# One group's shared-expert products moved behind the expert pairs, in a two-layer transformer block on one core

## The reference, cut to what matters

```python
def _L0_ffn_ref(x, gate_w, W1, W2, Ws1, Ws2):      # D 256, H 192, E 8, K 2, NS 2
    scores = jax.nn.softmax((xf @ gate_w.T).astype(jnp.float32), axis=-1)
    top_vals, top_idx = jax.lax.top_k(scores, K)
    w_dense = jnp.zeros((T, E), x.dtype).at[jnp.arange(T)[:, None], top_idx].set(weights)
    h = jnp.einsum('td,ehd->teh', xf, W1)
    y, g = jnp.split(h, 2, axis=-1)
    eo = jnp.einsum('teh,edh->ted', y * jax.nn.silu(g), W2)
    z = jnp.einsum('te,ted->td', w_dense, eo)
    z = z + _gated_mlp(xf, Ws1, Ws2)               # the shared expert, hidden width 384
    return z.reshape(x_shape)
x = L0_attn_x                                      # (2, 2048, 256) float32
x = _layernorm(x + _L0_attn_ref(x, L0_attn_w_qkv, L0_attn_w_conv1), axis=-1)
x = _layernorm(x + _L0_ffn_ref(x, ...), axis=-1)
```

## Time and profile before

| | |
|---|---|
| Device time, three runs | 361.57, 362.41, 365.29 us; median 362.41 us |
| Span of the profiled execution | 354.0 us (the time of that execution itself is not printed; the median lies 8.4 us above this span) |
| TensorE busy | 315.3 us, 89% of the span |
| VectorE busy | 265.5 us, 75% |
| ScalarE busy | 192.7 us, 54% |
| GpSimd busy | 197.5 us, 56% |
| Mean granted TensorE clock | 0.962 of full speed |

### The profile page before, as it was taken

One profiled execution on the slowest core, in us unless ns is written; L12 is line 12 of the kernel. 1 busy time (PEld: TensorE's weight loads), 2 busy tenths in 40 slices (PEclk: granted clock), 3 DMA queues, 4 the chain that ended last, 5 costly groups with the idle time before them and its releaser, 6 DMA issues.

```text
span 354.0 us, 7780 instructions
## 1 busy us (share of the span) xinstructions
PE 315.3 (89%) x2225; PEld 282.8 (80%) x2225; DVE 265.5 (75%) x1037; ACT 192.7 (54%) x425; POOL 197.5 (56%) x223
## 2 busy tenths in 40 slices
PE   2879899999999989999989979999999999999700
PEld 1446788789888878888889979999999999999600
DVE  0886679866989897966686765676678886988785
ACT  1043686646657362733335644555655566868862
POOL 4048750746778858667271542444757675686620
PEclk9969999999999999999999998999999999999955
DMA  7967420212371202442124643444899797789758
GB/s 221 378 220 262 126 62 0 95 47 75 101 216 58 92 33 93 114 136 101 35 98 140 191 144 100 129 131 131 178 247 204 202 243 190 177 236 252 204 189 324
DMA packets 31383, 54.63 MB, mean 154 GB/s; under 512 B 4880, under 2 KB 22544, under 8 KB 31344
## 3 DMA queue, kind: packets, MB, share of 16 engines
q1 hardware_dynamic: 23136, 29.82, 28.1%
q0 software_dynamic: 8208, 24.32, 23.9%
HBM read 29.73 MB, written 24.40 MB: 153 GB/s over the span
## 4 chain that ended last, share of the span: by engine, by line
PE 48%; DVE 16%; DMA 12%; SPq 8%; POOL 6%; issue 4%; ACT 4%; POOLq 0%; DVEq 0%; ACTq 0%
PE bank L1062 15%; PE bank L946 10%; PE bank L1088 8%; PE bank L968 4%; DMA stage<-ws_t 4%; PE bank L931 3%; PE bank L1071 3%; DMA stage<-rows_in 3%; PE bank L1031 3%; DVE xs L1174 3%; DVE htlo L1379 2%; SPq L415 2%; DVE mix L1374 2%; POOL rows_in L560 2%; POOL w1lo L516 2%
## 5 line engine op out<-in xcount | busy, mean ns | idle before, releaser
L600 POOL DMA_INDIRECT rows_out<-stage,place x71 | 69.4, 977 | 67.2 <-ACT stage L769 51.8
L560 POOL DMA_INDIRECT rows_in<-x,slot x64 | 65.3, 1020 | 47.1 <-DVE slot L1289 30.6
L749 ACT ACTIVATE stage<-bank 128x384 f32<-128x384 f32 (+1 forms) x36 | 17.5, 486 | 43.7 <-PE bank L1062 43.7
L1062 PE MATMUL bank<-w1hi,xthi 128*128 x142 | 39.8, 362 | 1.3 <-DVE xs L1385 1.1
L769 ACT ACTIVATE stage<-bank,weight 128x256 f32<-128x256 f32 x71 | 30.0, 471 | 15.8 <-PE bank L1088 15.7
L1062 PE MATMUL bank<-w1hi,xtlo 128*128 x142 | 36.9, 341 | 0.0
L1062 PE MATMUL bank<-w1lo,xthi 128*128 x142 | 36.8, 340 | 0.0
L1391 DVE TENSOR_TENSOR xtlo<-bank,xthi 128x512 fp32r<-128x512 f32 (+1 forms) x36 | 24.3, 676 | 13.7 <-ACT xthi L695 13.4
L1519 DVE TENSOR_TENSOR stage<-bank,stage 128x384 f32<-128x384 f32 (+1 forms) x36 | 19.8, 551 | 18.6 <-ACT stage L749 18.5
L687 ACT ACTIVATE mix<-bank 128x512 f32<-128x512 f32 x24 | 14.2, 591 | 34.1 <-PE bank L946 34.1
L946 PE MATMUL bank<-xthi,ws1hi 128*128 128x512 f32 x96 | 31.3, 407 | 0.0
(11 more groups left out here) (242 smaller groups left out, 893.4 us busy)
## 6 DMA issues: line engine op xcount, KB each, us to landing
stage<-rows_in SPq DMA_DIRECT2D x71, 133.0 KB, 2.6
xs<-rows_out POOLq DMA_DIRECT2D x12, 512.0 KB, 6.5
xs<-x SPq DMA_DIRECT2D x8, 512.0 KB, 9.2
out<-xs SPq DMA_DIRECT2D x7, 512.0 KB, 5.4
stage<-w_t SPq DMA_DIRECT2D x8, 384.0 KB, 4.4
rows_in<-clear SPq DMA_DIRECT2D x16, 133.0 KB
rows_out<-stage,place POOLq DMA_INDIRECT x71, 3.3
stage<-w_t SPq DMA_DIRECT2D x2, 512.0 KB, 3.9
```

The source lines that it names most:

```text
L560: pool.indirect_dma_start(rows_in[0:E * CAP, :], bass.IndirectOffsetOnAxis(slot[:, q * G + t, k:k + 1], 0), x2[q % 2][:, t, :], None).then ...
L600: pool.indirect_dma_start(rows_out[:, :], bass.IndirectOffsetOnAxis(place[:, 2 * j + b:2 * j + b + 1], 0), by[j % 4][:, b * C:(b + 1) * C] ...
L749: act.activation(bsg[j % 2][:, 0:width(j)], bank_h[j % 2][:, 0:width(j), H:F], ACT.Silu).then_inc(s_bsg, 1)
L1062: mm = pe.matmul(bank_h[j % 2][:, b, 0:F], bx[j % 2][:, (2 * b + k) * P:(2 * b + k + 1) * P], w[:, bass.ds(e, 1), k, :], start=(a == 0), s ...
```

## The change

Of group 7 only the routing stays ahead of the pairs. Its shared-expert products come after the last pair.

```diff
+LAST = NG - 1
-HIDDEN = 2
+HIDDEN = 4
+TABLE_AT = 4
     # TensorE
-            for g in range(NG):
+            for g in range(LAST):
                 group(g)
+            pe.wait_ge(s_xt, NG)
+            block_transposes(0)
+            logits_of(LAST)
+            block_transposes(1)
+            pe.wait_ge(s_pack, 1)
+            load_experts(0)
             pe.wait_ge(s_wlo, PIECES)
-            pe.wait_ge(s_slot, NG)
     # in its step
-                    if j == 2:
+                    if j == TABLE_AT:
                         spread_table(1)
                     if j == 1:
-                        for u in range(2):
-                            pe.wait_ge(s_zev[u], NG)
+                        pe.wait_ge(s_lsum, NG)
+                if i == 1:
+                    places(LAST)
+                    for u in range(2):
+                        pe.wait_ge(s_zev[u], LAST)
+                    if j == 0:
+                        pe.wait_ge(s_slot, NG)
             pairs(step)
+            last_group()
+            def last_group():
+                for m in range(MC):
+                    first_layer(LAST, m)
+                for m in range(2):
+                    pe.wait_ge(s_ht, hidden(LAST, m) + 1)
+                    for t in range(G):
+                        second_layer(LAST, t, [m])
+                close_group(LAST)
     # VectorE, before the pairs
+            block_lo(0)
+            route(LAST)
+            block_lo(1)
     # in its step
+                    if i == 1:
+                        tables(LAST)
+                        slots(LAST)
+                if i == 1:
+                    rest_blocks()
+                if i == 2:
+                    rest_regions()
                 if i == 3:
+                    rest_rows()
+                if i == TABLE_AT + 1:
                     pack_experts(slice(FULL // 4, NBK // 4))
+            def rest_blocks():
+                vec.wait_ge(s_slot, NG)
+                vec.tensor_copy(zrow[:], begin[0:1, :]).then_inc(s_ends, 1)
     # VectorE, behind the pairs
-            statistics(5, 1)
+            product(LAST, 0)
+            hidden_lo(LAST, 0)
+            scale_and_shift(2)
+            product(LAST, 1)
+            hidden_lo(LAST, 1)
+            gather(0)
+            product(LAST, 2)
+            hidden_lo(LAST, 2)
             statistics(6, 0)
-            scale_and_shift(2)
+            add_routed_input(LAST, 0)
             statistics(6, 1)
+            gather(1)
             scale_and_shift(3)
-            statistics(7, 0)
-            statistics(7, 1)
+            statistics(LAST, 0)
+            add_routed_input(LAST, 1)
+            statistics(LAST, 1)
             scale_and_shift(4)
     # ScalarE, behind the pairs
             finish_tiles(halves(3, 1))
-            deviations(2)
-            finish(4)
-            deviations(3)
+            for m in range(MC):
+                silu(LAST, m)
+                hidden_hi(LAST, m)
+                if m:
+                    finish_tiles(halves(4, m - 1))
+            act.preload_act_table(ACT.Sqrt)
             finish(5)
     # GpSimd
-                    26: (4, 1), 28: (5, 0), 30: (5, 1)}
+                    26: (4, 1), 28: (5, 0), 30: (5, 1), 32: (6, 0), 35: (6, 1)}
+            rough_rstd2(2)
+            rough_rstd2(3)
     # SP
-            store_groups(range(3))
+            store_groups(range(4))
             for u in range(2):
-                sp.wait_ge(s_zev[u], NG)
-            for n in range(2):
-                load_last(n, closed_pairs(NG - 1))
-            load_last(2, closed_pairs(HALF))
-            load_last(3, PAIRS)
-            store_groups([3, 4, 5, 6])
+                sp.wait_ge(s_zev[u], LAST)
+            load_last(0, closed_pairs(HALF))
+            load_last(1, PAIRS)
+            store_groups(range(4, LAST))
```

More of the change, by code:

```diff
@@ L224, in post_norm_layer, with last_results, sg, prod @@
         ln2 = [ln2t[:, n] for n in range(5)]
[L225 to L229, removed]
+        def last_results(h, k):
+            return mix[:, 2 * h + k, :].rearrange("p (t c) -> p t c", c=C)
+        def sg(g, m):
+            return work[:, m * GT:(m + 1) * GT] if g == LAST else mix[:, buf(g, m), :]
+        def prod(g, m):
+            return work[:, at_sg + m * GT:at_sg + (m + 1) * GT] if g == LAST else mix[:, 2 + buf(g, m), :]
         tokf = tok[:].rearrange("p b t -> p (b t)")
@@ L339, in buf, with gated, shared, logit_bank @@
             return hidden(g, m) % 2
+        def gated(g, m):
+            return (2 + 2 * m if m < 2 else 0) if g == LAST else 4 + 2 * buf(g, m)
+        def shared(g, u):
+            return (6 if g == LAST else 4 + 2 * buf(g, 1)) + u
+        def logit_bank(g):
+            return banks[5] if g == LAST else banks[2]
+        def place_bank(g):
+            return banks[7] if g == LAST else banks[2]
         def result(j, b):
@@ L711, in _ @@
                 silu(g, 1)
-                if g != 1 and g + 1 < NG:
+                if g != 1:
                     normalise(g + 1)
@@ L940, in first_layer @@
                     pe.wait_ge(s_row0, 1)
-                for h, (o, bank) in enumerate (((m * P, banks[4 + 2 * buf(g, m)]), (HS + m * P, banks[5 + 2 * buf(g, m)]))):
-                    if m == 0 and g:
+                for h, o in enumerate((m * P, HS + m * P)):
+                    bank = banks[gated(g, m) + h]
+                    if m == 0 and 0 < g < LAST:
                         pe.wait_ge(s_zev[h], g)
@@ L1442, in group @@
                     token_max(1)
-                if g + 1 == NG:
-                    vec.wait_ge(s_slot, NG)
-                    vec.tensor_copy(zrow[:], begin[0:1, :]).then_inc(s_ends, 1)
                 if g:
@@ L1562, in statistics, with gather @@
                 ins.then_inc(s_var, 1)
+            def gather(h):
+                tiles = slice(LAST * G + 2 * h, LAST * G + 2 * h + 2)
+                for k in range(K):
+                    before = xs[:, tiles, :] if k else x2[LAST % 2][:, 2 * h:2 * h + 2, 0:C]
+                    vec.wait_ge(s_last_in[h][k], 16)
+                    vec.tensor_tensor(xs[:, tiles, :], before, last_results(h, k), ALU.add).then_inc(s_last_x[k], 1)
+                    vec.wait_ge(s_last_x[k], h + 1)
             def scale_and_shift(n):
```

102 lines of the change are left out of this document (42 added, 60 removed).

## The result

| | changed | before | ratio |
|---|---|---|---|
| median of 4 runs each, us | 372.47 (370.98 to 378.58) | 362.14 (361.57 to 365.29) | 1.0265 [1.0213, 1.0316] |

The change makes the kernel 2.7% slower. Forecast were 363.0 us and a range to 367.0; it failed. Five further sets, each on one chip, came in two conditions.

What follows compares the result with a forecast made beforehand. Bound by TensorE in the pairs, then by a tail writing, reloading, adding and norming the last rows. Pairs end at 327.1 (7.9 us earlier) plus a 27.5 us tail: span 354.6, plus 8.4: 363.0 us, range 357 to 367.

Steps and rivals of the forecast that it cites:

- the front gives 7.9: Ahead of the pairs: pair 4's first load, and so the pairs' end, comes 7.9 us earlier, not 12.5.
- E: The end of the pairs' last matmul, 335.06 in the trace before, forecast at 327.1 after the change.
- both ways: Step from span to time: the median's 8.4 us above the span is added alike for both kernels.
- Part one: How much earlier the pairs end: SyncE's load list lets only 7.9 us of 12.5 through, TensorE idling at pairs 4 and 8.
- TensorE idle before them: Sign of being right: TensorE idles before the transposes of pair 8, near 202, forecast at 3.5 us.
- Part two: The tail behind the last pair's matmuls: follows VectorE's order and grows from 18.9 to 27.5 us.
- third rival: Tail: GpSimd's accumulating transfers land after over 9 us, delaying VectorE's wait for the power; 367.0 to 369.3 us, chance 0.17.
- The lower clock behind 2 us of idle: Tail: TensorE's last chunk takes 2.8 us for 1.4, VectorE's add waits 0.5 us; time would be 363.5.
- The front gives all: Rival at the front: pairs 0 and 8 start the full 12.5 us earlier; 358.4 us, chance 0.09.
- the tail follows TensorE: Rival in the tail: VectorE keeps up, so TensorE's 12.5 us of matmuls set the end; 354.8 us, chance 0.1.
- Late accumulating transfers: Rival in the tail: GpSimd's accumulating transfers land after over 9 us; 367.0 to 369.3 us, chance 0.17.
- The second table or the scatters hold up pair 8: Rival before pair 8's load: these come late despite 6.5 us of margin, each microsecond beyond costing one; chance 0.03.

Runs made afterwards that it cites:

- before_early: The kernel before, with SyncE loading pairs 4 and 5 ahead of its wait for the last group's counts; 360.31 us, 1.0023 of the kernel before.
- before_second: The kernel before, unchanged, run again for its profile in the slower condition; 363.0 us, 1.0024, span 362.0.
- loads_behind: The changed kernel, with SyncE waiting for all of group 7's scatters before pair 4's load instead of pair 8's; 378.11 us, 1.0435 of the kernel before.
- places_first: The changed kernel, with group 7's positions, tables, slots and `zrow` ahead of the first pair instead of in step 1; 369.65 us, 1.0217 of the kernel before.
- after_fourth: The changed kernel, unchanged, run a fourth time; 368.88 us, 1.0243 of the kernel before.
- early_loads: The changed kernel, with SyncE loading pairs 4 and 5 ahead of its wait for the last group's counts; 350.05 us, 0.9885 of the kernel before.
- early_rows2: early_loads, with the rest of the table's rows made in VectorE's step 2 instead of step 3; 348.59 us, 0.9868 of the kernel before.
- best_both: early_rows2, with GpSimd's power ahead of its last accumulating transfer and VectorE's step needing it behind all three low parts; 364.48 us, 1.014 of the kernel before.

## Why the prediction was wrong

**The step that failed: "the front gives 7.9".** Within the condition of the first result the front gives nothing. On set 3's chip E is 339.42 in before_early, which takes as long as the kernel before, and 340.72 in the change: minus 1.3 us. The tail takes 9.4 there (28.50 for 19.10), near the 8.5 of the forecast. In set 1 the same two terms are 8.8 (E 332.76 and 323.93) and 12.2 (30.46 for 18.25).

**How the sum came to miss it: its base.** "The profiled execution's own time is not printed; with the median's 8.4 above the span both ways." The 8.4 puts the kernel before where it was measured, and with 1.8 in its place the forecast would have been 356.4, further from 372.47. What is wrong is "both ways": the part of it inside the span is 8 to 11 us in the kernel before (362.0 against 354.0 and 351.0) and 15.1 in the change (369.5 against 354.4). What lies around the span is 1.8 us: 371.26 to 369.5 in the changed kernel, 352.78 to 351.0 and 363.81 to 362.0 in the one before. The other 6.6 us were inside the span, in executions unlike the one that I read. The trace of before, with its span of 354.0, shows what later executions of 353 to 356 us show; the runs beside it took 361.6 to 365.3. A gap of 8.4 us was the one sign in the material that the trace and the times belonged to two conditions, and I turned it into a constant.

**What lies in those 6.6 us.** Beside a row of scatters the other engines stand still on such chips, group scatters and rows of four in the pairs alike. So the front was mis-sized too, by "since rows 5 show the list without a gap" and by `slots`, routing and first weights at the durations of the earlier trace rows. The span in its parts, against the forecast (whose 20.5 and 4.6 are 20.7 and 4.45 in the earlier trace rows):

| | forecast | first result | same kernel, set 1 |
|---|---|---|---|
| logits of group 7 | 164.99 | 167.99 | 165.28 |
| pair 4's first load | 177.2 | 185.42 | 177.37 |
| from there to pair 8's load | 20.5 | 27.1 | 20.3 |
| from there to its transposes | 4.6 | 4.0 | 4.5 |
| from there to E | 124.8 | 125.2 | 121.8 |
| tail | 27.5 | 27.8 | 30.5 |
| span | 354.6 | 369.5 | 354.4 |

Of the 14.9 us between forecast and first result 3.0 arise before the logits, 5.2 more up to pair 4's load (of which TensorE shows 2.67 of idle at 173.10, 1.9 us behind group 6's last scatter, which ended at 171.23), 6.6 in SyncE's list, 0.3 in the tail.

**Why the kernel before loses less there.** Its span grows from 351.0 and 354.0 to 362.0, with pair 4's load at 189.16 instead of 185.12. Of the 8.0 us from the trace of 354.0, 0.6 lie before the logits, 3.5 up to that load, 1.4 in the list, 2.3 from pair 8's load to E and 0.4 in the tail. Beside group 6's scatters it has shared products, in which TensorE shows no wait over 0.7 us (before_second), and SyncE's list of loads begins when group 7's scatters are over. The change puts group 7's routing right behind group 6's scatters and SyncE's list, pair 0 to 2 and the table beside group 7's scatters, the two of pair 0 lengthening the row to ten. That the overlap costs SyncE's list 7 us is shown by loads_behind, whose 19.9 us stand against 27.0 to 27.3 in the other sets of this condition. That the rest of the excess has the same cause is read from where the standstills end, in the change, before_second and places_first, and not shown by an edit.

**Part one, mechanism**: right up to pair 4 where the kernel before takes 353 to 355 us. Both loads came within 0.2 us, and TensorE's idle at pair 4 was 3.07 against "some 3". Pair 8's transposes came at 202.11 against 202.3, but that is luck: they didn't wait for SyncE. The forecast had 3.5 us of idle there, and "TensorE idle before them" was its sign of being right. TensorE had spent that time earlier, in a wait that I had not listed, 1.81 us for the table before pair 4's weights, and at a lower clock behind the idle at pair 4 (0.62 granted in 184.20 to 186.90).

**Part two, the tail**: right in its order and within 0.3 us in the first result (27.8; 28.5 in after_fourth). In set 1 it was 3.0 longer, by the three late arrivals shown there. The first belongs to the third rival's place, VectorE's wait for the power, but not to its mechanism: it was the first transfer's wait for the scatters that came late (1.41 us), not its landing. The lower clock behind 2 us of idle was left out of the sum with 0.5 us; it was there with 0.80. The rule of the Trainium skill ("TensorE: Matmul & The Clock Gate", Part 1) is half rate after idle, and the trace agrees: 0.50 granted (the 1.2 GHz level) in 340.33 to 342.10, and in the first result too, where the 3.98 us of idle before pair 4 are followed by 4.10 us with 14 matmuls, and the 0.38 us before pair 8 by the full clock:

```profile
216.50:220.60 4.10, 4.09 (x30) 4.06 (x30) 1.75 (x5) 2.33 (x5) 1.91 (x2) 1.00 0.69 193
190.10:194.20 4.10, 4.10 (x14) 4.10 (x15) 0.00 (x0) 0.00 (x0) 3.19 (x4) 0.50 0.36 133
```
**The rivals.** None of them held the time. "The front gives all" and "the tail follows TensorE" were both ruled out as argued, by SyncE's list and by VectorE's. "Late accumulating transfers" gave 367 to 369.3, the right side for the wrong reason. "The second table or the scatters hold up pair 8" had 0.03 and named the scatters only by their landing, never as what slows others while they are issued. The second table did hold up pair 8 once, in places_first, by SyncE's wait of 5.5 us.

**The forecast's sum on its own ground.** 354.6 + 1.8 is 356.4; measured were 355.51 and 354.77, with ratios of 1.0036 and 1.0038 where 0.6 us of 354 is 1.0017. So the change is no gain even there, since the tail takes back what the front gives. With early_loads' list (1.2%) or early_rows2 (1.3%) it becomes one there; on the other kind of chip best_both, with that list, was 1.4% slower than the kernel before.

## What to carry to other kernels

When the span of the profile and the times of the runs are further apart than the start and the end of a program (1.8 us here), the trace is of another condition than the times: get a profile of the kernel before in that condition before working out a sum. Work that is cut away from between two rows of indirect scatters may be what kept the other engines busy beside them, as the traces here suggest; a kernel that lives from such an overlap should be timed on several chips, since the change with SyncE's list altered was 1.3% faster than the kernel before on one and, with two more edits, 1.4% slower on another. And SyncE's list of loads and zeroings is a resource like an engine: moving the loads of two pairs, which nothing held back, gave 5.5 us in set 1, where moving a group's shared products cost 1.2.

## What the runs showed of the hardware

On two of the five chips of these sets, and in the first result, SyncE's steps take 0.7 us each, and VectorE, ScalarE and TensorE stand still for 2 to 7 us, while GpSimd issues a row of eight to ten indirect scatters 1.27 us apart. GpSimd's own pace doesn't change (0.96 us each, 0.30 between them). All of it ends 1.3 to 2 us behind the last scatter: 196.2 for 194.23 and 173.1 for 171.23 in the change, 189.1 for 187.80 in the kernel before, 187.1 for 185.38 in places_first. On the other three chips the same kernels, with the same scatters, have no such stretch. Rows of four in the pairs do the same: in all eight traces of the slower condition ScalarE waits 2.5 to 3.7 us beside at least one of them, up to 0.8 to 1.1 us behind its last scatter (3.63 in before_second, 3.50 in after_fourth, 2.49 in the first result), and in none of the twelve of the faster condition does it wait over 1.6 us there. Scatters in twos mostly go without; in before_second SyncE's list is 1 us longer beside two such twos.

The Trainium skill ("SBUF — State Buffer", "SBUF: two separate sides") tells of a port that VectorE and GpSimd share, held by whichever starts first, and of GpSimd kept from writing its descriptors while VectorE holds it. That alone doesn't account for the trace: GpSimd keeps its 1.27 us while VectorE has nothing under way for 6.76 us, and SyncE and ScalarE, which are not part of that rule, wait too.

What it is in the chip, and whether it belongs to the chip or to the time of a set, stays open. Open is also whether the unbroken row does it or each scatter by itself; the runs with gaps fell on a chip that doesn't show it. No run here shows either whether an execution of which no trace is taken has these stretches.
